# Attention and a soft mixture of experts on one core: the 64 heads written out without a loop, and the work around four PSUM banks reordered

## The reference, cut to what matters

```python
# attention: 8 heads of 128, rotary embedding, causal
q, k, v = rope(x @ wq), rope(x @ wk), x @ wv
p = softmax(mask(q @ k.T / 128))
x = layernorm(x + sum_over_heads((p @ v) @ wo))
# soft mixture of experts: 8 experts of 64 slots, 512 slots in all
xn, se = rms_norm(x) * gamma_x, rms_norm(slot_embeds) * gamma_slot
logits = xn @ se.T                       # (1024 tokens, 512 slots)
dispatch = softmax(logits, over experts' axis of the slots)
slots = dispatch.T @ xn
processed = gelu(slots @ w1) @ w2
combine = softmax(logits, over all slots)
x = layernorm(x + combine @ processed)
```

## Time and profile before

| what | before |
|---|---|
| median of three runs | 1723.7 us (1721.98 to 1725.09) |
| profiled execution, own time | 1727.6 us |
| its span, first to last instruction | 1725.8 us |
| TensorE (PE) busy | 1657.2 us, 96% |
| weight loads (PEld) | 1483.8 us, 86% |
| VectorE (DVE) busy | 1218.4 us, 71% |
| ScalarE (ACT) busy | 1218.0 us, 71% |
| GpSimd (POOL) busy | 1420.9 us, 82% |
| mean granted TensorE clock | 0.990 |
| attention block | to 1429 us |

### The profile page before, as it was taken

How to read it: one execution, slowest core, us unless ns; L and a number is a source line. 1 busy time by engine, 2 the same in 40 slices (tenths; PEclk the granted TensorE clock), 3 DMA queues, 4 the chain that set the end, 5 groups by cost and what they waited for, 6 DMA issues and landing times. The chain is left out here.

```text
span 1725.8 us, 33880 instructions
## 1 busy us (share of the span) xinstructions
PE 1657.2 (96%) x10524; PEld 1483.8 (86%) x10524; DVE 1218.4 (71%) x2881; ACT 1218.0 (71%) x2425; POOL 1420.9 (82%) x812
## 2 busy tenths in 40 slices
PE   5999999999999999999999999999999997999996
PEld 4888888888888888888888888888888886889886
DVE  3677777776777777767777777777777775777764
ACT  3777777777777777767777777777777753655663
POOL 5889988997888888978999899988888865677775
PEclk9999999999999999999999999999999998999998
DMA  5223332232222322222223222322232323132211
GB/s 146 75 63 84 80 94 72 75 84 79 64 77 77 105 64 78 77 85 70 74 74 102 71 75 75 102 70 75 75 89 77 91 75 86 44 95 64 61 37 49
DMA packets 76520, 134.24 MB, mean 78 GB/s; under 512 B 19264, under 2 KB 45888, under 8 KB 76352
## 3 DMA queue, kind: packets, MB, share of 16 engines
q1 hardware_dynamic: 74880, 130.10, 27.9%
q10 hardware_dynamic: 1472, 2.10, 0.4%
HBM read 56.36 MB, written 8.70 MB: 38 GB/s over the span
## 5 line engine op out<-in xcount | busy, mean ns | idle before, releaser
L510 ACT ACTIVATE probs<-ps_slot,neg_max 128x640 f32<-128x640 f32 (+7 forms) x512 | 379.6, 743 | 143.6 <-DVE neg_max L628 143.6
L628 DVE CUSTOM_DVE_ANT_0 ps_slot<-ps_slot,causal 128x640 f32<-128x640 f32 (+7 forms) x512 | 385.6, 762 | 68.5 <-PE ps_slot L57 68.4
L844 PE MATMUL ps_turn<-ident,probs 128*128 128x128 f32 x2304 | 322.7, 275 | 17.9 <-DVE x_t L681 7.2
L844 PEld LDWEIGHTS ps_turn<-ident,probs 128*128 128x128 f32 x2304 | 259.1, 140 | 42.0 <-DVE x_t L681 8.8
L55 PE MATMUL ps_slot<-k,q 128*128 128x512 f32 (+4 forms) x768 | 282.0, 367 | 3.1 <-ACT unrot_q L531 1.4
L57 PE MATMUL ps_slot<-k,q 128*128 128x512 f32 (+4 forms) x768 | 264.5, 344 | 0.0
L56 PE MATMUL ps_slot<-k,q 128*128 128x512 f32 (+4 forms) x768 | 263.4, 343 | 0.0
L655 DVE TENSOR_TENSOR pt_split<-ps_turn,pt_split 128x512 fp32r<-128x512 f32 x256 | 175.6, 686 | 93.3 <-ACT pt_split L555 93.3
L655 DVE TENSOR_TENSOR pt_high<-ps_turn,pt_high 128x128 fp32r<-128x128 f32 (+3 forms) x256 | 124.6, 487 | 119.8 <-ACT pt_high L555 119.8
L423 POOL TENSOR_TENSOR swapped_k<-swapped_k,rope 128x1024 f32<-128x1024 f32 x64 | 154.2, 2409 | 61.6 <-DMA swapped_k<-unrot_k 61.6
L439 POOL TENSOR_TENSOR q<-rot_q,q 128x1024 fp32r<-128x1024 f32 x64 | 154.0, 2406 | 61.7 <-ACT q L538 61.7
(11 more groups left out here) (168 smaller groups left out, 4311.8 us busy)
## 6 DMA issues: line engine op xcount, KB each, us to landing
swapped_k<-unrot_k SPq DMA_DIRECT2D x128, 256.0 KB, 3.6
swapped_q<-unrot_q SPq DMA_DIRECT2D x128, 256.0 KB, 3.7
inv_b<-inv_rows SPq DMA_DIRECT2D x64, 512.0 KB, 4.4
x_rows<-in_L_attn_x SPq DMA_DIRECT2D x8, 512.0 KB, 5.6
y_t<-y_sum SPq DMA_DIRECT2D x8, 512.0 KB, 5.2
x_rows<-y_t SPq DMA_DIRECT2D x8, 512.0 KB, 3.9
unrot_q<-in_L_attn_x SPq DMA_DIRECT2D x8, 512.0 KB, 5.0
row_b<-r_rows SPq DMA_DIRECT2D x16, 256.0 KB, 3.6
```

The lines of the kernel that those rows point to most:

```text
L510: act.activation(probs_tile(t), score_tile(name, head, i), ACT.Exp, scale=-1.0, bias=neg_max[:, head.par, t:t + 1], accum_out=sums[:, head ...
L628: dve.tensor_tensor_reduce(tile, tile, causal[:, T - WIDTH[t]:T], -1.0, UNSEEN, ALU.add, ALU.min, neg_max[:, head.par, t:t + 1]).then_inc( ...
L844: last = pe.transpose(bank[:, at:at + P], probs_tile(t)[:, j * P:(j + 1) * P], ident[:, :])
```

## The change

`steps` becomes a Python loop: the 48 steps of the three turns are written out, and every wait of the attention block is for a constant. `wait_apart` adds its increment only where the value is a register's, so the increments vanish from the whole attention block, from batch 0 and from what follows the second block's loop. TensorE's `weigh_high(before, (2, 3))` stands ahead of the two waits and of `s7`. In the second block the tokens are turned into the two banks of `ps_acc`. In batch 0 tiles 2 to 5 are turned into the four banks of `ps_slot`, so that only tiles 6 and 7 wait for a row peak, and the slot sums are placed between the turned tiles. In the other batches `sum_slots(1)` comes after `turn_tile(2)`. At the end, batch 6's output rows are made by VectorE, and GpSimd makes the norm for them between two pairs of `sub_rows`; batch 7 goes to `res` and to `last_out`, which is batch 6's `x1`, and its rows are shared out anew. The diff, without the lines that only pass `first` on or name a tile or a semaphore:

```diff
@@ -61,7 +61,8 @@
 
 
     eng.wait_ge(sem, value)
-    eng.sem_inc(ticks, 1)
+    if not isinstance(value, int):
+        eng.sem_inc(ticks, 1)
 
 
 def f32(ap):
...
@@ -299,7 +300,7 @@
 
             for at in range(0, 2):
                 step(Head(0, at, heads))
-            with eng.Fori(0, heads // 16 - 1) as loop:
+            for loop in range(heads // 16 - 1):
                 for at in range(2, 18):
                     step(Head(loop, at, heads))
             for at in range(2, last + 1):
...
@@ -943,11 +944,11 @@
                 if is_step(head, heads - 1):
                     pe.wait_ge(tokens_added, 1)
                 scores("s4", head)
+                weigh_high(before, (2, 3))
                 if after.live():
                     pe.wait_ge(raw_made[0], after.made() * 2)
                     pe.wait_ge(cos_made[0], after.made() * 2)
                 scores("s7", head)
-                weigh_high(before, (2, 3))
                 turn("3", before, ("2", before))
                 turn("10", before, ("5a", before))
                 free_slot(exped[4], head)
...
@@ -1000,7 +1001,7 @@
 
 
 
-FFN_TURN = {"proc": 0, "tok0": 1, "tok1": 0, "z0": 1, "z1": 0, "slots": 1}
+FFN_TURN = {"proc": 0, "z0": 1, "z1": 0, "slots": 1}
...
 
-        def tile_bank(t):
+        def token_bank(half):
+            return ps_acc[:, half, :]
+
+        def tile_bank(t, first):
+
+            if first and 2 <= t < 6:
+                return ps_slot[:, (t - 2) // 2, (t - 2) % 2 * BANK:((t - 2) % 2 + 1) * BANK]
             return ps_turn[:, (t + 1) % 2, :]
 
         def token_cols(t):
...
@@ -1143,10 +1152,10 @@
             batch(B - 2, 0, False, True, False)
             batch(B - 1, 1, False, True, False)
             store(B - 2)
-            for half, (made, value) in enumerate(((out_made, (B - 1) * NT + NT // 2 + 1), (last_rows, NT // 2))):
+            for half, made in enumerate((first_rows, last_rows)):
                 tiles = half_tiles(half)
-                sp.wait_ge(made, value)
-                sp.dma_start(out[B - 1, :, :].rearrange("(t p) m -> p t m", p=P)[:, tiles, :], out_row[:, tiles, :])\
+                sp.wait_ge(made, NT // 2)
+                sp.dma_start(out[B - 1, :, :].rearrange("(t p) m -> p t m", p=P)[:, tiles, :], last_out[:, tiles, :])\
                   .then_inc(out_free, 16)
             sp.wait_ge(out_free, 16 * (B + 1) + 1)
 
...
@@ -1187,11 +1196,12 @@
                                               rstd[:, 0, t:t + 1], ALU.add, ALU.mult)
                 last.then_inc(x1_made, 1)
 
-            def sub_rows(b, par, half, first):
-                wait_apart(pool, row_landed[half], b * 16 + 16, ticks)
-                if not first:
-                    wait_apart(pool, out_summed, b * 4 - 2 * (1 - half), ticks)
-                for c in range(NC):
+            def sub_rows(b, par, half, first, chunks=range(NC)):
+                if 0 in chunks:
+                    wait_apart(pool, row_landed[half], b * 16 + 16, ticks)
+                    if not first:
+                        wait_apart(pool, out_summed, b * 4 - 2 * (1 - half), ticks)
+                for c in chunks:
                     out, src = (rows.rearrange("q (t p) -> q t p", t=4) for rows in
                                 (comb[:, c, half_cols(half)], logits[par][:, c, half_cols(half)]))
                     pool.tensor_tensor(out, src, row_b[:, half, :].rearrange("q (p t) -> q t p", t=4),
...
@@ -1221,15 +1231,21 @@
             with pool.Fori(0, B // 2 - 1) as pair:
                 batch(pair * 2 + 1, 1, False, True)
                 batch(pair * 2 + 2, 0, False, True)
-            batch(B - 1, 1, False, False)
-            wait_apart(pool, out_free, (B - 1) * 16 + 1, ticks)
-            for half, made in enumerate((out_made, last_rows)):
+            Steps.at = ahead_of_one
+            last_base = (B - 2) * per_batch
+            sub_rows(B - 1, 1, 0, False)
+            sub_rows(B - 1, 1, 1, False, range(2))
+            second_norm(B - 2, last_base)
+            pool.sem_inc(last_norm_known, 1)
+            sub_rows(B - 1, 1, 1, False, range(2, NC))
+            for half, (made, rows) in enumerate(((first_rows, (0, 1)), (last_rows, (4, 6)))):
                 wait_apart(pool, half_stats_b, half + 1, ticks)
-                kept.mean_rstd(pool, counted((B - 2) * per_batch), 1, half_tiles(half))
+                if half == 0:
+                    wait_apart(pool, out_made, (B - 1) * NT + 1, ticks)
+                kept.mean_rstd(pool, counted(last_base), 1, half_tiles(half))
                 pool.sem_inc(half_normed, 1)
-
-                for t in range(half * NT // 2, (half + 1) * NT // 2, half + 1):
-                    pool.tensor_scalar(out_row[:, t, :], res2[:, t, :], neg_mean[:, 1, t:t + 1],
+                for t in rows:
+                    pool.tensor_scalar(last_out[:, t, :], res[:, t, :], neg_mean[:, 1, t:t + 1],
                                        rstd[:, 1, t:t + 1], ALU.add, ALU.mult).then_inc(made, 1)
 
         @block.scalar
...
@@ -1299,7 +1315,7 @@
                 dve.wait_ge(in_landed, b * 32)
                 dve.wait_ge(x1_made, b * 2)
                 dve.wait_ge(tokens_turned, b * 2 - (1 - half))
-                dve.tensor_tensor(res[:, half_tiles(half), :], turn(f"tok{half}").rearrange("p (t m) -> p t m", m=D),
+                dve.tensor_tensor(res[:, half_tiles(half), :], token_bank(half).rearrange("p (t m) -> p t m", m=D),
                                   x_row[:, half_tiles(half), :], ALU.add).then_inc(added1, 1)
 
             def row_stats(src, which, done, value, done_a, done_b, tiles=slice(0, NT)):
...
@@ -1357,16 +1373,18 @@
                 dve.wait_ge(proc_summed, b + 1)
                 dve.tensor_copy(proc[:, :, 0:D], turn("proc").rearrange("p (c d) -> p c d", d=D)).then_inc(proc_copied, 1)
 
-            def add2(b, par, q):
+            def add2(b, par, q, last_batch=False):
+                to = res if last_batch else res2
                 dve.wait_ge(out_summed, b * 4 + (q + 1))
                 dve.wait_ge(x1_made, b * 2 + (q // 2 + 1))
-                dve.wait_ge(out_made, b * NT + 1)
+                if not last_batch:
+                    dve.wait_ge(out_made, b * NT + 1)
                 sums = out_bank(q)[:, 0:2 * D1].rearrange("p (t d) -> p t d", d=D1)
                 dve.reciprocal(inv_out[:, 2 * q:2 * q + 2], sums[:, :, D]).then_inc(out_inverted, 1)
                 dve.wait_ge(out_inverted, b * 4 + (q + 1))
                 for i in range(2):
                     t = 2 * q + i
-                    last = dve.scalar_tensor_tensor(res2[:, t, :], sums[:, i, 0:D], inv_out[:, t:t + 1],
+                    last = dve.scalar_tensor_tensor(to[:, t, :], sums[:, i, 0:D], inv_out[:, t:t + 1],
                                                     x1[par][:, t, :], ALU.mult, ALU.add)
                 last.then_inc(added2, 1)
 
...
@@ -1415,16 +1433,22 @@
                 batch(pair * 2 + 2, 0, False, True)
             batch(B - 1, 1, False, False)
             copy_proc(B - 1)
+            dve.wait_ge(last_norm_known, 1)
+            dve.wait_ge(out_free, (B - 2) * 16 + 1)
+            for t in range(NT):
+                dve.tensor_scalar(out_row[:, t, :], res2[:, t, :], neg_mean[:, 1, t:t + 1],
+                                  rstd[:, 1, t:t + 1], ALU.add, ALU.mult).then_inc(out_made, 1)
+            dve.wait_ge(out_made, (B - 1) * NT + 1)
             for half in range(2):
-                add2(B - 1, 1, 2 * half)
-                add2(B - 1, 1, 2 * half + 1)
+                add2(B - 1, 1, 2 * half, True)
+                add2(B - 1, 1, 2 * half + 1, True)
                 dve.wait_ge(added2, (B - 1) * 4 + (2 * half + 2))
-                row_stats(res2, 1, None, half + 1, half_stats_a, half_stats_b, half_tiles(half))
-            dve.wait_ge(half_normed, 2)
-            dve.wait_ge(out_free, (B - 1) * 16 + 1)
-            for t in range(NT // 2 + 1, NT, 2):
-                dve.tensor_scalar(out_row[:, t, :], res2[:, t, :], neg_mean[:, 1, t:t + 1],
-                                  rstd[:, 1, t:t + 1], ALU.add, ALU.mult).then_inc(last_rows, 1)
+                row_stats(res, 1, None, half + 1, half_stats_a, half_stats_b, half_tiles(half))
+            for half, (made, rows) in enumerate(((first_rows, (2, 3)), (last_rows, (5, 7)))):
+                dve.wait_ge(half_normed, half + 1)
+                for t in rows:
+                    dve.tensor_scalar(last_out[:, t, :], res[:, t, :], neg_mean[:, 1, t:t + 1],
+                                      rstd[:, 1, t:t + 1], ALU.add, ALU.mult).then_inc(made, 1)
 
         @block.tensor
         def _(pe):
...
@@ -1448,11 +1472,13 @@
                                         z_t[:, 0, half_cols(half)], z_t[:, 1, half_cols(half)], True, True)
                 last.then_inc(logits_in, 1)
 
-            def turn_tile(b, par, t):
-                if t >= 2:
+            def turn_tile(b, par, t, first):
```

(50 more changed lines are left out.)

29 lines of the change are left out of this document (15 added, 14 removed).

## The result

| what | before | after |
|---|---|---|
| median | 1723.7 us (1721.98 to 1725.50, 5 runs) | 1693.96 us (1692.21 to 1695.32, 5 runs) |
| ratio, 95% interval | | 0.9825 (0.9811 to 0.9839) |
| profiled execution, own time | 1727.6 us | 1695.3 us |
| its span | 1725.8 us | 1693.5 us |
| mean granted TensorE clock | 0.990 | 0.994 |

The forecast was 1693.0 us, the range 1686 to 1704. The span is 32.3 us shorter, the medians differ by 29.8: the profiled execution of the kernel before lies 3.9 us above its median, that of the kernel after 1.4. Later the changed kernel was run once more and gave 0.9828.

What follows compares the result with a forecast made beforehand. TensorE was taken to set the time nearly everywhere, so only its lost time counted. Terms 8.6 + 6.5 + 8.7 + 3.5 + 3.5 = 30.8 us off the 1723.7 us median gave 1693 us, range 1686 to 1704.

Steps and rivals of the forecast that it cites:

- The loop written out: Attention block: writing out the loop removes two turns back of 4.3 us each, 8.6 us (bounds 5.4 and 9.5).
- Rival 1: Attention block: straight code's instruction fetches show, making the kernel slower, 1741 us; chance 0.03.
- Rival 2: Attention loop: the turn back is cheap and the 2.5 us idle has another cause that stays, 1702 us; chance 0.06.
- Straight steps: Attention block: a written out step takes 0.05 us more than a looped one, lost at tile 7's scores.
- High products ahead of `s7`: Attention steps: moving these products ends tile 7's late start and slow first matmul, 6.5 us with the first steps.
- no 0.47 at the first matmul of `s7`: Sign in the attention steps: the first matmul of tile 7's scores no longer takes 0.47 us.
- Increments: Attention block: they stood on engines that wait for TensorE, so leaving them out was taken to give nothing.
- Batches 1 to 6: Second block: tokens in `ps_acc` end waits for `proc` and `add1`, 1.45 us a batch, 8.7 us (bounds 3 and 9.6).
- at 15.5 us: Sign in the second block: the stretch from turned tokens to turned z rows takes 15.5 us, from 17.0.
- Rival 3: Second block: the peaks' landing or the z scale takes the 8.7 us back, 1702 us; chance 0.12.
- Batch 0: Second block's first batch: without waits for tiles, slot rows are turned earlier, 3.5 us (bounds 2 and 4.5).
- The end: After batch 7's output sums begin: VectorE makes eight rows in 2.2 us, last norm starts earlier, 3.5 us (1.5 to 4.3).

Runs made afterwards that it cites:

- e1: Kernel before with only the 48 looped attention steps written out, increments kept: 1719.4 us, ratio 0.9968.
- e9: Changed kernel with the second block's loop of three turns written out as well: 1695.3 us, ratio 0.9826 to the kernel before.
- e5: Kernel before with the first of the attention loop's three turns written out, so it turns back once: 1724.3 us, ratio 0.9994.
- e3: Kernel before with only the high products of j = 2, 3 moved ahead of tile 7's scores, loop kept: 1721.8 us, ratio 0.9979.
- e4: Changed kernel with the high products put back behind tile 7's scores: 1703.2 us, ratio 0.9871 to the kernel before.
- e2: Kernel before with the attention loop written out and increments behind waits for constants left out: 1716.7 us, ratio 0.9952.
- e8: Kernel before with only tokens turned into the accumulation banks and tile 1's slot sums behind turned tile 2: 1718.6 us, ratio 0.9959.
- after_again: The changed kernel itself, unaltered, run once more: 1695.5 us, ratio 0.9828 to the kernel before.
- e6: Changed kernel without batch 0's four extra banks, batch 0 in the other batches' order: 1698.2 us, ratio 0.9840 to the kernel before.
- e10: Changed kernel with GpSimd's last two subtractions ahead of batch 6's norm, so VectorE makes its rows alone: 1697.6 us, ratio 0.9831 to the kernel before.
- e7: Kernel before with only the end changed (batch 6's rows on VectorE, norm between subtractions, batch 7's own buffers): 1721.3 us, ratio 0.9979.

## Why the prediction was right, step by step

**The loop written out.** Predicted 8.6 us for two turns back. The longer steps of the kernel before give 4.1 and 4.5 (the prediction took 4.3 for both, against two steps of 21.21; the second step of the pair takes 21.43 where no loop turns). e1 shows them gone, with no cluster of fetches in their place. Rival 1, that the straight code's fetches show, fell with the same runs: no plain step behind step 2 of any straight kernel is longer than 21.28 us, and e9 has 13 more fetches at no cost. Rival 2, the cheap branch, fell in this block, since what e1 takes away is the turn back alone. The missing distinction was between loops: the price comes with fetching the body again, and where no fetch is seen, as in the second block, the turn is free. What the prediction had no row for is that the price varies with the build: 6.8 us in e5, of which 2.3 are a second stop.

By the windows of the earlier trace rows TensorE issues 1490 + 1488 matmuls and weight loads for six middle batches, so some 990 for the two batches of a turn, and 2042 + 2041 in 15.6 steps, so some 4200 for the 16 steps of a turn. Waits and branches are not in these counts. The loop whose turn is free is the one with the short body; no run tried another length, so that length is the reason is argued from these two loops.

The Trainium skill, "Runtime: NRT & Kernel Launch", section "Instruction fetch mechanics", gives TensorE a store of 2048 instructions, and says that a taken branch whose target lies outside the pages held has to fetch it first. The traces agree with the 2048: a body of some 990 is not fetched again and one of 4200 is. They don't agree with the same section's words that those pages are the current two, of 256 instructions each: by these the body of 990 would be fetched again too. The same skill's branch time of 108 ns ("Advanced Engine Details and Errata", "Control Flow Timing") can stand for the first kind of turn, and is short of the second kind's price by 3.8 us or more.

**Straight steps.** That they take 0.05 us more than looped ones, as the steps from 50 on do in the kernel before, holds in e1: 48 of them cost 2.7 us back. The prediction put this into the next part, and there the size was off.

**High products ahead of `s7`: mis-sized.** The step that failed is "Its first matmul also takes 0.47 us where the next takes 0.40, since its weights couldn't be loaded ahead", with the conclusion that both this and the late start go away: 0.09 a looped and 0.15 a straight step, 6.5 us. Measured: 0.04 (e3) and 0.08 (e4). The late start went. The slow first matmul stayed at 0.28 to its successor instead of 0.31, probably since what now stands ahead of it are the shortest matmuls of the step, 0.06 to 0.12 us apart beside weight loads of 0.19; the prediction's own mark, "no 0.47 at the first matmul of `s7`", is met by 0.44 and so hardly at all. That the load lags because of the short matmuls is read from the rows, not tried by an experiment. (Also behind the turned tiles, transposes of 128 columns, a matmul of 512 columns is followed only after 0.31 us: 381.35 to 381.66 in the kernel after.) In steps 2 to 62 the two parts gave 11.3 us together where the terms make 8.6 + 48 x 0.09 + 12 x 0.15 = 14.7.

**Increments.** 0 in the attention block is right (steps 2 to 62 take 1294.2 us in e1 and 1294.0 in e2).

**Batches 1 to 6.** Predicted 8.7, measured 8.6 in the profiled kernel, 7.2 in e8 and 6.6 to 8.1 in five others that have the same order and banks (after_again, e4, e6, e9, e10). The cause was named in part: the prediction gave the whole 1.5 us a batch to the waits for `proc` and `add1`, and passed over the wait for ScalarE's exponential, 1.5 of the 4.3 us that TensorE waits in these batches of the kernel before. The stretch "at 15.5 us" is met in four of six batches. Rival 3, the next bound, is real in part: batches 2 and 3 of the kernel after wait 0.2 and 0.7 us at a row peak. The z scale and the peaks' landing seem to take back up to 2 us of the gain, which fits a slack that was put at 0.2 us and at nothing.

**Batch 0.** Predicted 3.5, measured 4.0; 9.14 us from first peak to slot rows, predicted 9.5. e6 shows the mechanism. The segment as a whole is less steady: it varies between 40.0 and 42.5 us in the builds that have the change, and 43.5 to 46.3 in those that don't.

**The end.** Predicted 3.5, measured 4.1, within its bounds. VectorE's rows took 1.7 us longer than the term had them, so additions begin 3.8 us after the sums and not within 3. It cost nothing there, as VectorE catches up before the last sum: its last reciprocal, ahead of the last two additions, begins 0.04 us behind TensorE's end (0.12 us in e10, with the rows undisturbed but later). In e7 it begins 0.48 behind, so there it did cost some tenths.

Here the Trainium skill's rule ("SBUF — State Buffer", "SBUF: two separate sides": whichever of VectorE, in certain modes, and GpSimd starts first holds the shared ports for the whole instruction) got the effect right. GpSimd's pair started first and kept its 3.02 us. The prediction applied the rule with GpSimd as the loser, which made it an argument about the third output sum; the loser was VectorE, 1.3 to 2.3 us in six builds.

**The sum.** The terms had 15.1 for the attention block; 11.3 came from its steps. The profiled span shows 4.1 more at its start and at the passage to the second block, and these are mostly not the change. Among all builds, with and without it, the start takes 66.4 to 69.7 us, and the passage 57.3 to 57.8, and 59.4 in two (the kernel before and e8). Both go with stretches of 3.4 us in which TensorE's clock is at 0.50, up to 1.7 us each: the two builds with three of them in the start take 69.6 and 69.7 us, the two with one 66.4 and 67.0, the others, with two, 66.6 to 68.5; and only the two with 59.4 us have one inside the passage, at 1399 and 1398 us. The kernel before has seven half-clock stretches ahead of its last output sum, the kernel after four (one of them in the last row of the first fence above). Whether the change makes them fewer was not tried. Against this, 2.5 of the 32.3 us are only the choice of the two profiled executions, as the medians show. So the right total has a part of luck: about 3.4 us too much for the move, made up by about 1 us in batch 0 and at the end, and by this.

## What to carry to other kernels

Price a loop's turn from its own place in the trace: look there for clusters of instruction fetches. Where they are, writing the loop out gave some 4 us or more a turn for a few hundredths a step; where no fetch is seen, it gave nothing. A bank that is free at the right time is worth looking for: two `ps_acc` banks, with one slot sum moved, gave 7 us and four `ps_slot` banks 3. When you cost a matmul that comes late, take start to next start, and look at what the new neighbour does to its weight load.

## What the runs showed of the hardware

- A turn back with fetches costs TensorE 3.9 to 6.8 us (nine turns in five builds); a turn back without, nothing that shows.
- GpSimd's two subtractions stretch eight rows of VectorE from 2.14 to between 3.46 and 4.41 us, by holding the first two rows until they end, and are not stretched themselves.
- A small operation of GpSimd that waits for the one before it starts 0.1 us sooner when no increment stands between (2.10 against 1.81 us for a chain of four starts).
- Behind stretches in which TensorE is idle for a good part (busy 1.56 of the 4 us ahead of 1430 us in the kernel before) it is granted half its clock, 1.2 of 2.4 GHz, for 3.4 or 6.8 us: at the start, at the blocks' passage, in batch 0, and at three of the turns back. Where this falls differs from build to build; the passage takes 59.4 us with such a stretch at 1398 and 57.3 to 57.8 without.
